# The head of a fused attention and expert kernel in another order, with the norm's statistics in a third piece

## The chip, the cores and the metric

The kernel runs as one program on one core of a Trainium2 chip. The metric is device time in microseconds. The kernel before has a median of 527.07 us over three runs, from 525.77 to 527.6.

## The reference

The reference is a gated cross-attention layer followed by a mixture-of-experts layer, all in 32-bit floats: 8 batches of 256 queries (`x`, width 256), 120 context rows per batch, 16 heads of 64, 8 experts with a hidden width of 1024, of which each token takes two.

```python
q = (layernorm(x) @ w_q).reshape(b, n, 16, 64)
k, v = split((ctx @ w_kv).reshape(b, m, 2, 16, 64))
out = softmax(einsum('bnhd,bmhd->bhnm', q, k) * 64 ** -0.5) @ v
x = x + tanh(g_xattn) * (out @ w_out + b_out)
probs = softmax(layernorm(x) @ Wr.T)            # 2048 tokens, 8 experts
gate = top-2 of probs, scaled to sum to one
y = sum over experts e of gate_e * (silu(xn @ W1[e].T) @ W2[e].T)
x = x + tanh(g_ffn) * y
```

## The kernel before, in words

Every 32-bit factor is split into a high part and a low part of 16 bits, and a product is three 16-bit products. ScalarE (ACT) makes the high parts, VectorE (DVE) or GpSimd (POOL) the low ones. The parts carry a power of two that is found on the chip: ACT or DVE takes a bound of a tensor (`weight_max`), PE spreads it (`attn_maxima`, bounds Actx, Awk, Awq, and A3 for the two that come last), and DVE makes the scale of it (`attn_scales`). The first batch doesn't wait for the split: its Q and K products take the 32-bit tensors as they are (`plain`, L1713).

Eight batches go through a software pipeline. Each engine has a loop `for p` (SP L511, POOL L741, ACT L1027, DVE L1565, PE L2020) whose body is a list of calls with an offset: `row_max(p + 2, 0)` acts on batch p + 2 in round p and does nothing outside 0 to 7. A function that works once returns where its batch is not 0. So the lists are an order written out by hand, and an engine runs its list strictly in that order; what it waits for are semaphores. The round of a batch is about 31 us long. The products share three banks (`j_bank`); four tables (`PRODUCT_ORDER`, `FULL_ORDER`, `HIGH_ORDER`, `FREE_ORDER`) tell in which order banks are taken, filled and freed, and from them come the semaphore counts.

What the change touches:

- `filler` (L1725): matmuls of a constant that keep PE busy. `x_T` (L1742) turns the normed queries of a batch; `x_high` (ACT, L833) and `x_low` (DVE, L1224) split them. For batch 0, `x_low` (L1245) leaves one 32-bit copy, `xn2T`. `q_product` and `k_product` make four parts of Q and two of K; `row_scores` (L1908) makes scores whose row maxima `row_max` (L1389) takes.
- `weight_sum` (ACT, L927): sums of squares of an expert's two weight matrices for the scale of their split, two instructions of 2048 elements each; `weight_diagonals` (L952) and the reduction of the spread sums (L1315) follow, and every split of these weights waits for them.
- `x_stats` (DVE, L1144 and L1147): mean and variance of the query tiles of 128 rows. There are 16: two for batch 0, then four, then ten.
- `norm_factors` (POOL, L565 to L573): eight small instructions that make scale and shift of the norm for the tiles of one piece. ACT norms batch b (L905) when its piece is done.
- `p_low` (POOL, L618): the low part of the softmax numerators, which PE's products with V wait for. `scatter` (L637): a batch's routes into a table in memory. `norm2_factors` (L647): the second norm's factors. POOL also makes low parts of the expert weights (L663 to L667).

```python
RESTS = ((NT, 4), (NT + 4, TT - NT - 4))      # tiles in the pieces after the first
SUMS = (1, 3,)                                # bounds that ACT takes as sums of squares
```

After the eighth round only the work on expert tiles is left, the last 29 of 39 in a loop of their own (`step`).

## Time and profile before

| | |
|---|---|
| median of three runs | 527.07 us (525.77 to 527.6) |
| the profiled execution | 530.4 us, of which the span is 528.7 us |
| mean granted TensorE clock | 0.983 |
| instructions | 17694 |
| PE busy | 486.9 us, 92% |
| DVE busy | 363.8 us, 69% |
| ACT busy | 371.2 us, 70% |
| POOL busy | 369.9 us, 70% |
| chain that ended last | PE 66%, POOL 12%, DVE 9%, ACT 5%, issue 5%, DMA 3% |

The span is the time between the first and the last instruction that the profiler saw; the profiled execution's time is 1.7 us more. Times on the timeline count from the span's start. The shares are means over stages that differ: up to some 75 us PE has gaps, afterwards hardly any, and from some 300 us on only expert tiles are left. Releasers are inferred, and a busy PE is not PE at its peak.

### The profile page before, as it was taken

Reading aid. Unit: us, or ns where it says so; the run is one execution under the profiler, and the core shown is the slowest. Engines: PE = TensorE matmul, PEld = TensorE weight load, DVE = VectorE, ACT = ScalarE, POOL = GpSimd, SP = SyncE. Lnnn points to the kernel's source line nnn. Section 1 sums busy time; section 2 is a strip of 40 time slices with the busy share of each in tenths; the row PEclk is TensorE's granted clock in tenths of the full one; section 3 lists DMA queues with packets and bytes.
Section 4 is the critical chain, followed back from the end, with each engine's and each line's share of the span. In section 5 each row is a group of like instructions: output and inputs, shape, how many; then the busy total and the mean of one; then the engine's idle time right before and its main releaser. Section 6 shows DMA issues by size and latency. Waiting matters only on the chain.

```text
span 528.7 us, 17694 instructions
## 1 busy us (share of the span) xinstructions
PE 486.9 (92%) x6692; PEld 436.4 (83%) x6692; DVE 363.8 (69%) x866; ACT 371.2 (70%) x577; POOL 369.9 (70%) x414
## 2 busy tenths in 40 slices
PE   2889689999999999999688999989999999999993
PEld 2877568888888878888468899979999999999993
DVE  5799899898988989998887757553344443444431
ACT  1788989999899989988764577544555655556551
POOL 5369779798999999899968766564554645455432
PEclk9999989999999999999989999998999999999998
DMA  7953416154360725325073638886888888788712
GB/s 289 398 195 95 167 38 204 51 185 140 99 208 34 243 67 182 124 95 195 24 268 110 255 118 303 251 254 150 260 226 245 241 226 265 212 256 239 211 22 31
DMA packets 35061, 94.87 MB, mean 179 GB/s; under 512 B 4507, under 2 KB 24475, under 8 KB 27645
## 3 DMA queue, kind: packets, MB, share of 16 engines
q1 hardware_dynamic: 25812, 82.79, 45.2%
q0 software_dynamic: 8592, 10.81, 11.9%
q8 instruction: 57, 0.93, 0.7%
q14 instruction: 24, 0.20, 0.1%
q10 hardware_dynamic: 576, 0.14, 0.1%
HBM read 74.45 MB, written 19.28 MB: 177 GB/s over the span
## 4 chain that ended last, share of the span: by engine, by line
PE 66%; POOL 12%; DVE 9%; ACT 5%; issue 5%; DMA 3%; POOLq 0%; SPq 0%; ACTq 0%; DVEq 0%
PE st_bank L1707 20%; PE j_bank L1707 15%; PE o_bank L1707 14%; PE j_bank L1852 4%; POOL pT L618 3%; POOL stage L663 3%; PE max_pair L1908 2%; PE j_bank L1713 2%; PE st_bank L1929 2%; POOL table L637 2%; PE j_bank L1811 2%; DMA stage<-in_w 2%; PE max_pair L1970 1%; DMA w2s<-in_wq 1%; PE j_bank L1876 1%
## 5 line engine op out<-in xcount | busy, mean ns | idle before, releaser
L1541 DVE SCALAR_TENSOR_TENSOR hT<-hf,h_scale,hT 128x512 f16<-128x512 f32 x78 | 58.9, 758 | 87.2 <-ACT hT L1016 87.1
L1707 PE MATMUL st_bank<-xsT,w_tile 128*128 128x128 f16 x1872 | 113.3, 221 | 2.1 <-DVE xsT L1535 1.4
L1707 PEld LDWEIGHTS st_bank<-xsT,w_tile 128*128 128x128 f16 x1872 | 109.6, 99 | 3.0 <-DVE xsT L1535 1.6
L730 POOL DMA_INDIRECT out<-yt,row_of x39 | 62.7, 1607 | 57.0 <-DVE yt L1550 42.3
L1010 ACT ACTIVATE hf<-st_bank,z_scale 128x512 f32<-128x512 f32 x78 | 52.9, 678 | 45.2 <-PE st_bank L1707 39.2
L618 POOL TENSOR_TENSOR pT<-pT 120x512 f16<-120x512 f32 x64 | 77.3, 1223 | 7.3 <-ACT pT L884 7.1
L1707 PE MATMUL o_bank<-w2s,hT 128*128 x600 | 69.7, 273 | 0.3 <-DVE yt L1550 0.3
L1016 ACT ACTIVATE hT<-hf,h_scale 128x512 f16<-128x512 f32 x78 | 56.3, 722 | 10.5 <-PE o_bank L1707 4.2
L1707 PEld LDWEIGHTS o_bank<-w2s,hT 128*128 128x128 f16 x600 | 57.6, 98 | 7.1 <-issue 0.8
L883 ACT ACTIVATE pT<-st_bank,exp_bias,logit_scale 120x512 f32<-120x512 f32 x64 | 50.0, 781 | 14.0 <-PE st_bank L1932 12.7
L663 POOL TENSOR_SCALAR stage<-stage,upw 128x512 f32<-128x512 f32 x32 | 56.5, 1766 | 4.1 <-ACT w_hi L983 4.1
L710 POOL DMA_INDIRECT xg<-xn,row_of x39 | 40.6, 1041 | 14.3 <-issue 11.0
L884 ACT ACTIVATE pT<-st_bank,exp_bias,logit_scale 120x512 f16<-120x512 f32 x64 | 50.1, 782 | 0.0
L1852 PE MATMUL j_bank<-wos,oT 128*128 128x256 f16 x384 | 45.5, 272 | 1.0 <-DVE oT L1224 1.0
L1707 PE MATMUL j_bank<-xnT,wqs 128*128 128x256 f16 x336 | 41.4, 274 | 1.7 <-DVE oT L1224 1.6
L1707 PE MATMUL o_bank<-v,pT 120*128 120x65 f16 x768 | 34.2, 194 | 8.4 <-DVE o L1412 5.5
L1707 PEld LDWEIGHTS o_bank<-v,pT 120*128 120x128 f16 x768 | 29.5, 98 | 15.0 <-issue 12.2
L991 ACT ACTIVATE xsT<-max_pair 128x256 f16<-128x256 f32 x39 | 14.8, 380 | 37.7 <-PE max_pair L1970 37.6
L1852 PEld LDWEIGHTS j_bank<-wos,oT 128*128 128x128 f16 x384 | 36.3, 98 | 5.3 <-DVE oT L1224 1.2
L637 POOL DMA_INDIRECT table<-entry,slot x32 | 32.2, 1005 | 11.0 <-issue 7.4
L1707 PE MATMUL j_bank<-w2s,hT 128*128 x336 | 39.0, 273 | 0.0
L1707 PEld LDWEIGHTS j_bank<-xnT,wqs 128*128 128x128 f16 x336 | 31.9, 98 | 6.5 <-DVE oT L1224 1.8
(226 smaller groups left out, 1022.7 us busy)
## 6 DMA issues: line engine op xcount, KB each, us to landing
w_tile<-w_split SPq DMA_DIRECT2D x39, 1024.0 KB, 6.3
stage<-in_w SPq DMA_DIRECT2D x16, 1024.0 KB, 5.1
w_split<-w_hi SPq DMA_DIRECT2D x8, 512.0 KB, 2.8
w_split<-stage SPq DMA_DIRECT2D x8, 512.0 KB, 3.8
out<-x SPq DMA_DIRECT2D x17, 128.0 KB, 3.2
xin<-in_x SPq DMA_DIRECT2D x8, 256.0 KB
w2s<-in_wkv SPq DMA_DIRECT2D x2, 1024.0 KB, 11.9
xres<-in_x SPq DMA_DIRECT2D x16, 128.0 KB, 2.1
```

Of the source, the lines that this page charges most:

```text
L618: pool.tensor_tensor(pT[g % 2][:, 1, h, :], pT32[:, h, :], pT[g % 2][:, 0, h, :], ALU.subtract).then_inc(pT_low[h], 1)
L637: pool.indirect_dma_start(out=table[:], out_offset=bass.IndirectOffsetOnAxis(slot[b % 2][:, t, k:k + 1], 0), in_=entry[b % 2][:, t, k, :], ...
L663: chain.link(pool.tensor_scalar(chunk, chunk, upw[q % 2][:, i:i + 1], None, ALU.mult))
L710: pool.indirect_dma_start(out=xg[t % XG][:], out_offset=None, in_=xn2_dram[0:rows], in_offset=bass.IndirectOffsetOnAxis(row_of[:, t:t + 1] ...
L730: pool.indirect_dma_start(out=out[0:rows], out_offset=bass.IndirectOffsetOnAxis(row_of[:, t:t + 1], 0), in_=yt[t % XG][:], in_offset=None, ...
L883: nc.scalar.activation(pT32[:, h, :], st_bank[h][0:M, :], ACT.Exp, bias=exp_bias[0:M], scale=logit_scale[0:M])
L884: nc.scalar.activation(pT[g % 2][:, 0, h, :], st_bank[h][0:M, :], ACT.Exp, bias=exp_bias[0:M], scale=logit_scale[0:M]).then_inc(exp_done[h ...
L1010: nc.scalar.activation(hf[par][:, cols], z_bank[a][:], ACT.Silu, scale=z_scale[:, bass.ds(t, 1)]).then_inc(silu_done, 1)
L1016: nc.scalar.activation(hT[par][:, 0, 4 * a:4 * a + 4, :], hf[par][:, cols].rearrange("p (c n) -> p c n", c=4), ACT.Copy, scale=h_scale[:, ...
L1541: nc.vector.scalar_tensor_tensor(out=hT[par][:, 1, 4 * a:4 * a + 4, :], in0=hf[par][:, 512 * a:512 * a + 512].rearrange("p (c n) -> p c n" ...
L1707: ins = pe.matmul(out, lhs[i](a), rhs[i](c), start=(i == 0 and a + c == 0), stop=(i == n - 1 and a == 1))
L1852: ins = pe.matmul(dst[:, 0:D], oT[t][:, a, ic, :], wos[:, c, ic, :], start=(ic + a + c == 0), stop=(ic == IC - 1 and a == 1))
```

## The change

- PE's head: 100 fillers first, then the queries of batch 0 are turned, and the bounds Awq, Actx and Awk are spread each with one Q product of batch 0 behind it. K's product and the first scores follow; A3 comes later, behind the transposition of the second batch's queries.
- DVE, ACT and POOL follow that order in the head: DVE takes its 32-bit copy of the turned queries ahead of its constants, and the row maxima of the first scores, the bound of the output weights and several low parts ahead of A3's scale. The bound of the context moves from DVE to ACT, where it becomes a sum of squares (`SUMS`). POOL's memset of the pads waits for the scale of `w_q`, and a quarter of the context's low part moves ahead of the first norm factors.
- ACT: `x_high` stands ahead of both `weight_sum`s, in every round.
- The third piece of the norm is split in two: four tiles at its old place, and the last six later. DVE's statistics for them come in round 1, behind `norm2_rows(0)`, POOL's factors in round 2, among the first scatters.
- The tables of banks have entries of their own for batch 0. From round 6 on the lists are written out without a loop, in the same order.

On PE, at the program's start; `o_bank<-onesb` is a filler, `w2s,onesb` the spreading of a bound, `ident,xin` the transposition, `xn2T,w2s` the Q products, `xn_0,w2s` K's. Before:

```order
L1725 MATMUL o_bank<-onesb 128x128 x12
L1838 MATMUL j_bank<-w2s,onesb 128x128
L1742 MATMUL j_bank<-ident,xin 128x128 x4
L1725 MATMUL o_bank<-onesb 128x128 x40
L1838 MATMUL j_bank<-w2s,onesb 128x128
L1725 MATMUL o_bank<-onesb 128x128 x16
L1838 MATMUL j_bank<-w2s,onesb 128x128
L1713 MATMUL j_bank<-xn2T,w2s 128x256 x12
L1713 MATMUL j_bank<-xn_0,w2s 128x120 x16
L1838 MATMUL j_bank<-w2s,onesb 128x256
L1908 MATMUL max_pair<-kT,qT 128x120 x24
```

And now:

```order
L1901 MATMUL o_bank<-onesb 128x128 x100
L1918 MATMUL j_bank<-ident,xin 128x128 x4
L2012 MATMUL j_bank<-w2s,onesb 128x128
L1889 MATMUL j_bank<-xn2T,w2s 128x256 x4
L2012 MATMUL j_bank<-w2s,onesb 128x128
L1889 MATMUL j_bank<-xn2T,w2s 128x256 x4
L2012 MATMUL j_bank<-w2s,onesb 128x128
L1889 MATMUL j_bank<-xn2T,w2s 128x256 x4
L1889 MATMUL j_bank<-xn_0,w2s 128x120 x16
L2082 MATMUL max_pair<-kT,qT 128x120 x24
```

Two of the three Q products now stand ahead of the last of the three bounds, one behind it, and A3 (128x256) is gone from ahead of the scores.

On DVE in round 1, behind the copy of the first batch's turned second norm (`xn2T<-j_bank`). Before:

```order
L1226 SCALAR_TENSOR_TENSOR qT<-j_bank,qT 128x512
L1309 COPY xn2T<-j_bank 128x512
L1409 RECIPROCAL rsum<-o_bank 128x4
L1412 TENSOR_TENSOR o<-o_bank,rsum 128x2x2x64
L1226 SCALAR_TENSOR_TENSOR qT<-j_bank,qT 128x512
L1335 MAX top<-j_bank 128x8 x2
```

And now:

```order
L1331 SCALAR_TENSOR_TENSOR qT<-j_bank,qT 128x512
L1414 COPY xn2T<-j_bank 128x512
L1249 BN_STATS stats<-w2s 128x6 x6
L1252 BN_AGGR mv<-stats 128x2 x6
L1514 RECIPROCAL rsum<-o_bank 128x4
L1517 TENSOR_TENSOR o<-o_bank,rsum 128x2x2x64
L1331 SCALAR_TENSOR_TENSOR qT<-j_bank,qT 128x512
L1440 MAX top<-j_bank 128x8 x2
```

Twelve instructions on six tiles stand between the copy and the attention's work.

On POOL in round 2, at the first batch's scatters (`table<-entry,slot`). Before:

```order
L618 TENSOR_TENSOR pT<-pT 120x512
L637 DMA table<-entry,slot 16512x16 x2
L618 TENSOR_TENSOR pT<-pT 120x512
L637 DMA table<-entry,slot 16512x16 x2
L647 TENSOR_SCALAR ln_b<-mv 128x2
```

And now:

```order
L626 TENSOR_TENSOR pT<-pT 120x512
L645 DMA table<-entry,slot 16512x16 x2
L626 TENSOR_TENSOR pT<-pT 120x512
L572 TENSOR_SCALAR ln_a<-mv 128x6
L573 TENSOR_TENSOR ln_a<-ln_a,minus_half 128x6
L574 TENSOR_TENSOR ln_a<-ln_a 128x6
L575 TENSOR_TENSOR ln_a<-ln_a 128x6
L576 TENSOR_SCALAR ln_a<-ln_a 128x6
L577 TENSOR_SCALAR ln_a<-mv 128x6
L579 TENSOR_TENSOR ln_scale<-ln_a 128x6
L580 TENSOR_TENSOR ln_shift<-ln_a,ln_scale 128x6
L645 DMA table<-entry,slot 16512x16 x2
```

Eight instructions on six columns stand between a low part and the second pair of scatters, and all that follows on POOL comes behind them.

The core of the diff:

```diff
-RESTS = ((NT, 4), (NT + 4, TT - NT - 4))
-SUMS = (1, 3,)
+RESTS = ((NT, 4), (NT + 4, 4), (NT + 8, TT - NT - 8))
+SUMS = (0, 1, 3)
...
-PRODUCT_ORDER = (("Awq", 4), ("Q3", 2), ("X2T", -1), ("Q1", 2), ("LG", -1), ("FE", -2), ("Ka", 2), ("Vb", 1), ("OT0a", 0),
+PRODUCT_ORDER = (("XTf", 4), ("Awq", 4), ("Q3", 2), ("X2T", -1), ("Q1", 2), ("LG", -1), ("FE", -2), ("Ka", 2), ("Vb", 1), ("OT0a", 0),
...
-            sp.dma_start(x_rest[1], x_v[:, RESTS[1][0]:sum(RESTS[1]), :]).then_inc(x_all_in[1], 16)
+            for i in range(1, len(RESTS)):
+                sp.dma_start(x_rest[i], x_v[:, RESTS[i][0]:sum(RESTS[i]), :]).then_inc(x_all_in[i], 16)
...
+                pool.wait_ge(up_done[2], 1)
                 pool.memset(pad, 0.0).then_inc(pool_chain, 1)
...
                 p_low(p + 6, 2, 1)
+                norm_factors(p + 6, 2)
+                norm_factors(p + 4, 3)
                 scatter(p + 4, 1)
...
+                weight_low(p + 8, 0, 0, 0, 1)
                 norm_factors(p + 8, 1)
-                weight_low(p + 8, 0, 0)
+                weight_low(p + 8, 0, 0, 1, WEIGHT_PARTS)
...
-                norm_factors(p + 7, 2)
                 p_low(p + 7, 2, 0)
...
                 exps(p, 2, 1)
+                x_high(p + 2)
                 weight_sum(p + 1, 0)
-                x_high(p + 2)
...
                 x_stats(p + 1, 2)
                 norm2_rows(p - 1)
+                x_stats(p - 1, 3)
...
+                first_x_low(p + 3)
+                constants(p + 3)
                 attn_scales(p + 3, 0)
+                first_q_low(p + 3, 0)
...
                 row_max(p + 2, 0)
+                weight_max(p + 2, 4)
...
+            def first_x_T(b):
+                if b == 0:
+                    filler(100)
+                    x_T(b)
+
+            def first_q(b, i):
+                if b == 0:
+                    q_product(b, i)
...
-                attn_maxima(p + 2, 3)
...
-                x_T(p + 3)
+                x_T(p + 3 if p > -3 else B)
+                attn_maxima(p + 2, 3)
...
+                first_q(p + 3, 0)
                 attn_maxima(p + 3, 0)
+                first_q(p + 3, 3)
```

## Rows read from the trace of the kernel before

**Rows 1.** Chain of waits: start us, us on the chain, what.

```profile
74.52 2.79 PE j_bank L1707 x24
...
177.55 1.35 POOL w2s L667
```

**Rows 2.** Busy time in windows: stretch, length, five engines, PEclk, DMA, GB/s.

```profile
80.00:100.00 20.00, 20.00 (x305) 17.33 (x302) 17.72 (x44) 18.90 (x31) 15.54 (x20) 1.00 0.48 156
122.00:178.00 56.00, 54.60 (x822) 47.60 (x820) 50.71 (x126) 51.75 (x81) 52.28 (x55) 1.00 0.39 125
28.20:38.50 10.30, 8.85 (x138) 7.20 (x139) 9.89 (x20) 8.91 (x12) 7.35 (x6) 1.00 0.55 190
62.90:66.20 3.30, 0.73 (x14) 0.47 (x14) 2.68 (x6) 3.21 (x7) 0.87 (x1) 1.00 0.00 0
68.00:69.00 1.00, 1.00 (x3) 0.22 (x1) 0.96 (x3) 0.84 (x3) 0.82 (x2) 0.50 0.00 0
```

**Rows 3.** Timeline of the head: start us, us, engine, line, operation, [idle before <-releaser].

```profile
13.31 1.91 ACT L938 ACTIVATE w_hi<-w2s 128x2048 f16<-128x2048 f32 x1 [3.14 <-DMA w2s<-in_wkv]
...
16.51 1.06 PE L1725 MATMUL o_bank<-onesb 128*128 128x128 bf16 x16
...
17.40 0.22 PE L1838 MATMUL j_bank<-w2s,onesb 128*128 128x128 bf16 x1
...
19.10 5.42 PE L1713 MATMUL j_bank<-xn2T,w2s 128*128 128x256 f32 x24 [1.48 <-DVE xn2T L1245]
...
24.07 2.28 DVE L1155 TENSOR_REDUCE amax<-w2s 128x1 f32<-128x2048 f32 x1
...
24.36 3.73 PE L1713 MATMUL j_bank<-xn,w2s 128*128 128x120 f32 x32
...
28.12 0.80 PE L1908 MATMUL max_pair<-kT,qT 64*128 64x120 f16 x24
...
38.51 1.28 DVE L1212 SCALAR_TENSOR_TENSOR wkvs<-w2s,up,wkvs 128x1024 f16<-128x1024 f32 x1
```

**Rows 4.** Timeline of 45 to 66 us, DVE and ACT.

```profile
45.45 3.35 DVE L1144 BATCH_NORM_STATS2 stats<-w2s 128x6 f32<-128x256 f32 x10
...
48.84 0.78 DVE L1147 BATCH_NORM_AGGREGATE mv<-stats 128x2 f32<-128x6 f32 x10
...
50.10 0.60 ACT L850 ACTIVATE v<-j_bank 120x512 f16<-120x512 f32 x1 [1.20 <-PE j_bank L1713]
...
60.92 1.96 ACT L927 ACTIVATE w2s<-stage 128x2048 f16<-128x2048 f32 x1
...
63.49 0.69 DVE L1224 TENSOR_TENSOR xnT<-j_bank,xnT 128x512 f16<-128x512 f32 x1 [2.26 <-ACT xnT L833]
...
65.44 0.70 ACT L952 ACTIVATE diag<-ident,amc 128x128 bf16<-128x128 f32 x2
```

**Rows 5.** Timeline of 106 to 114 us, DVE and PE.

```profile
106.51 0.68 DVE L1309 COPY xn2T<-j_bank 128x512 f32<-128x512 f32 x1
...
112.43 0.68 DVE L1224 TENSOR_TENSOR oT<-j_bank,oT 128x512 f16<-128x512 f32 x1
...
113.44 1.42 PE L1707 MATMUL j_bank<-ctxs,wkvs 128*128 128x120 f16 x24
```

**Rows 6.** Timeline of POOL, with one PE row.

```profile
57.52 0.27 POOL L565 TENSOR_SCALAR ln_a<-mv 128x10 f32<-128x10 f32 x1
...
61.49 2.27 POOL L618 TENSOR_TENSOR pT<-pT 120x512 f16<-120x512 f32 x2
...
122.13 1.22 POOL L637 DMA_INDIRECT table<-entry,slot  x1 [0.55 <-DVE entry L1369]
...
128.35 0.23 POOL L647 TENSOR_SCALAR ln_b<-mv 128x2 f32<-128x2 f32 x1
...
130.93 2.72 POOL L618 TENSOR_TENSOR pT<-pT 120x512 f16<-120x512 f32 x2
...
133.75 0.53 PE L1707 MATMUL o_bank<-v,pT 120*128 120x65 f16 x12 [0.73 <-issue]
```

More of the change, by code:

```diff
@@ L127, in positions @@
     @staticmethod
-    def positions(order, without=None):
+    def positions(order):
         at = {}
@@ L137, in bank @@
     def bank(self, name, b):
-        return self.taken[name, b] % JOB_BANKS
+        return self.taken[job(name, b), b] % JOB_BANKS
     def fulled(self, name, b):
-        return self.full[name, b] + 1
+        return self.full[job(name, b), b] + 1
     def highed(self, name, b):
-        return self.high[name, b] + 1
+        return self.high[job(name, b), b] + 1
     def freed(self, name, b):
-        return self.free[name, b] + 1
+        return self.free[job(name, b), b] + 1
 JOBS = Jobs()
@@ L667, in split_low, with weight_low @@
                     pool.tensor_tensor(w2_part(q, 1, c), chunk, w2_part(q, 0, c), ALU.subtract).then_inc(w2_low[k], 1)
-            def weight_low(b, i, j):
+            def weight_low(b, i, j, first, last):
                 if b:
@@ L678, in weight_low @@
                 n = (hi - lo) // WEIGHT_PARTS
-                for c in range(0, hi - lo, n):
+                for c in range(first * n, last * n, n):
                     part = raw[:, :, c:c + n]
@@ L977, in split_high @@
                     elif q < 6:
-                        for j in range(2):
+                        for j in range(len(RESTS)):
                             act.wait_ge(stats_done[j], 1)
@@ new lines, in _ @@
+            exps(6, 1, 0)
+            o_high(5, 1, 1)
+            exps(6, 1, 1)
+            o_high(5, 0, 1)
+            k_high(7, 1)
+            gate_ratio(4)
+            q_high(7, 2)
+            exps(6, 2, 0)
+            exps(6, 2, 1)
+            weight_sum(7, 0)
+            weight_sum(7, 1)
+            weight_diagonals(7)
+            exps(6, 3, 0)
+            exps(6, 3, 1)
+            split_high(7, 0, 0)
+            o_high(6, 1, 0)
+            v_high(7, 0)
+            split_high(7, 0, 1)
@@ new lines, in _ @@
+            norm2(5)
+            split_high(7, 1, 1)
+            exps(7, 0, 0)
+            exps(7, 0, 1)
+            split_high(7, 1, 0)
+            v_high(7, 1)
+            o_high(6, 0, 0)
+            exps(7, 1, 0)
+            o_high(6, 1, 1)
+            exps(7, 1, 1)
+            o_high(6, 0, 1)
+            gate_ratio(5)
+            exps(7, 2, 0)
+            exps(7, 2, 1)
+            exps(7, 3, 0)
+            tile_high(7, 0)
+            exps(7, 3, 1)
+            tile_high(7, 1)
@@ new lines, in _ @@
+            split_low(7, 0, 2)
+            norm2_rows(5)
+            norm_o(6, 3, 1)
+            choose(5)
+            row_max(7, 3)
+            row_ids(4, 0)
+            tile_experts(4, 0)
+            v_low(7, 1)
+            o_low(6, 0, 0)
+            norm_o(7, 0, 0)
+            split_low(7, 1, 1)
+            o_low(6, 1, 1)
+            max_rows(7, 1)
+            split_low(7, 1, 0)
+            norm_o(7, 0, 1)
+            tile_scales(7, 0, 0)
+            o_low(6, 0, 1)
+            slots(5)
@@ new lines, in _ @@
+            tile_T(7, 0)
+            tile_T(7, 1)
+            spare('OT1a', 7, 44)
+            values(7, 2, 0)
+            tile_up(7, 0, 0)
+            o_T(7, 1, 0)
+            tile_up(7, 0, 1)
+            values(7, 2, 1)
+            tile_up(7, 1, 0)
+            values(7, 3, 0)
+            norm2_T(6)
+            values(7, 3, 1)
+            logits(6)
+            o_T(7, 0, 0)
+            o_T(7, 1, 1)
+            tile_up(7, 1, 1)
+            o_T(7, 0, 1)
+            ranks(6)
+            out_product(7, 1, 0)
@@ new lines, in _ @@
+            out_product(7, 1, 1)
+            out_product(7, 0, 0)
+            tile_T(7, 2)
+            out_product(7, 0, 1)
+            tile_T(7, 3)
+            tile_down(7, 0)
+            tile_up(7, 2, 0)
+            tile_T(7, 4)
+            tile_down(7, 1)
+            tile_T(7, 5)
+            norm2_T(7)
+            tile_up(7, 2, 1)
+            logits(7)
+            tile_up(7, 3, 0)
+            tile_up(7, 3, 1)
+            ranks(7)
+            tile_down(7, 2)
+            tile_up(7, 4, 0)
```

499 lines of the change are left out of this document (298 added, 201 removed).

## The prediction, on record before the changed kernel ran

> **What bounds the kernel now.** I read the chain of waits first. Its last piece on PE before the stage in which PE is full is the group of Q products at 74.52 us; from there it runs over PE and, from 122 us on, over POOL's splits of the expert weights, of which the last is at 177.55 [rows 1]. Then I read busy time by windows [rows 2]. Between 80 and 100 us PE is busy 20.00 of 20 us. Between 122 and 178 PE is busy 54.60 of 56 and POOL 52.28, and POOL's gaps there are short waits at scatters such as the 0.55 at 122.13 [rows 6]. So the kernel has three stages that matter here: a head to about 75 us in which PE has gaps (0.73 us busy between 62.9 and 66.2), a stage in which PE is full, and one in which PE and POOL are both nearly full. What is won in the head is carried through the later stages, since they have no slack to swallow it and nothing in them waits for a fixed time. What is added to an engine in the later stages is paid unless a slack is there in that place.
>
> In the head DVE and ACT set the pace: from 28.2 to 38.5 DVE is busy 9.89 of 10.30 us and ACT 8.91, PE 8.85 [rows 2]. Behind 50 us it is ACT: it waits 1.20 us for a V product at 50.10 [rows 4], and in the window at 63 us it is busy 3.21 of 3.30 while DVE is 2.68 and POOL 0.87.
>
> **The head, to the low part at 38.51.** K's product of the first batch needs the bound of the K weights. They land at 13.31 us, after ACT waited 3.14 for the transfer, and the bound is spread at 17.40 [rows 3]. Neither moves: the transfer and ACT's pass over it are the same. But before, three Q products stood between bound and K, 5.42 us for 24 records, and they started only at 19.10, because DVE made their operand late. Now two of them come before the bound and one is left behind it: 5.42 / 3 = 1.81. So K starts at about 17.4 + 0.2 (the spreading) + 1.8 and some wait for the scale, which I put at 0.3: 19.7 instead of 24.36. From K's start to the end of the first scores before is 28.12 + 0.80 - 24.36 = 4.56 us, of which some 0.2 was A3's spreading, which is now later. The first row maxima can thus start at 19.7 + 4.4 = 24.1. Behind them DVE has the same set of work as before from 28.2 to 38.5, which is 10.30, and the bound of the output weights (2.28 at 24.07 [rows 3]) with its diagonal of some 0.2, which moved behind the row maxima: 24.1 + 10.3 + 2.5 = 36.9. The same low part starts at 38.51 before. That is **-1.6 us**. The other edits of the head are in that set: the bound of the context goes from DVE to ACT, where a wait of 3.14 for a transfer hides it, and the memsets and the quarter of a low part on POOL stand where POOL has a gap.
>
> **The split of the statistics, its gain.** Ten tiles cost DVE 3.35 + 0.78 = 4.13 us at 45.45 and 48.84 [rows 4]; four cost 0.4 of it, 1.65, so DVE saves 2.48 there. It is not all gain, since ACT limits this stretch: what ACT can use of it is the 1.20 that it waited for the V product at 50.10, which stands behind DVE's work. I take **-1.2**; the bounds are 0 and -2.5.
>
> **The high part ahead of the weight sums.** The transposed queries' high part stood behind a sum of 1.96 us at 60.92, and DVE waited 2.26 for it at 63.49. Now DVE gets it earlier, but the two sums still have to be done on ACT before the diagonals at 65.44 [rows 4], for which the weights' split waits, and they come no earlier: ACT does the same work in another order. I take **0**, with bounds 0 and -2.3.
>
> **The statistics' six tiles in round 1.** They cost 0.6 of 4.13 = 2.5 us in one piece on DVE, directly behind the copy at 106.51 [rows 5]. PE is full there, and what DVE does next frees the banks into which PE writes. The slimmest place shown is that of a low part that ends at 112.43 + 0.68 = 113.11 and frees a bank for the K product at 113.44: a slack of 0.33 us. A slack of that size leaves 2.5 - 0.3 = 2.2 of the burst for PE to wait; some of DVE's idle time is in between (the copy's end at 107.19 to the next operation), so I take **+2.0**. The bounds are 0, if PE can go on with work whose banks are free, and 2.5.
>
> **The factors' eight instructions in round 2.** Two sizes are in the trace: eight instructions on two columns take 130.93 - 128.35 = 2.58 us, on ten columns 61.49 - 57.52 = 3.97 [rows 6]. Six columns lie midway: 3.3. POOL is nearly full from 122 us on, and PE waits for it: 0.73 us at 133.75 for the low parts that ended just before [rows 6]. Behind the eight instructions stand the second pair of scatters, the second norm's factors, the low parts for which PE waits there, and the weights' splits on which the chain of waits ends. I take **+3.3**; the bounds are 0, if POOL's own slack is larger than it looks, and 3.3. The piece at the old place shrinks from ten columns to four, which saves at most a microsecond there, but POOL has gaps in that stretch (0.87 of 3.30 busy at 63 [rows 2]), so it gives nothing.
>
> **The sum.** -1.6 - 1.2 + 0 + 2.0 + 3.3 = +2.5 us. Against the profiled execution, 530.4 us (a span of 528.7 and 1.7 around it), this makes 532.9. That execution lies 3.3 us above the median of 527.07, and the median is what the next runs are like, so I forecast 527.07 + 2.5 = 529.6.
>
> **The rivals.** *Both moved pieces are hidden (faster).* The mechanism is that POOL's eight instructions displace nothing that PE needs at once: they stand behind the low part of 122 us and before scatters whose result is read rounds later, and the low parts behind them could come 2.6 us later than now if the engines ahead of PE had that much stored. Then DVE's burst is taken up in the same way, and only the head's -2.8 is left: 524.3. For it speaks that PE's wait in this place is only 0.73 us; against it that POOL has no more than 56 - 52.28 = 3.7 us of gaps in the whole stretch [rows 2]. It decides if PE's waits for low parts in round 2 stay under one microsecond.
>
> *All gains of the head add (no change).* If DVE, not ACT, sets the pace to 75 us, the 1.6 of the head, the 2.5 of the statistics and the 2.3 of the high part add to 6.4, and with the 5.3 that the moved pieces cost the time is 527.07 - 6.4 + 5.3 = 526.0. For it speaks DVE's wait of 2.26; against it ACT's 3.21 of 3.30 in the same window. If the gains add and the pieces are hidden too, it would be 520.7; I give that little.
>
> *The head's PE slows down (slower).* Now PE does its 100 fillers in one piece at the start: at the 1.06 us for 16 of [rows 3] they take 6.6 us and end before the queries are there to be turned, and a gap follows in which PE has next to nothing. The row of 62.9 to 66.2 shows such a gap, and in the row of 68 to 69 the granted clock is 0.50, the lower of its two levels, 1.2 GHz of 2.4 [rows 2]. If that happens before the Q and K products, the Q product behind the bound takes 1.81 more, and the head's 1.6 is gone. Then the sum is -1.2 + 5.3 = +4.1, or 531.2. The Trainium skill has a rule on this ("TensorE: Matmul & The Clock Gate", Part 1: The HAM clock gate): the clock follows how busy the engine has lately been, and an engine that pauses goes back to half rate. The trace agrees with it in those two windows. By that rule alone the gap behind the fillers would decide for this rival; against it stands that the bounds and Q products now follow one another closely.
>
> **How the numbers follow.** What one measurement of this kernel can't tell from no change is about 0.3%, 1.6 us: faster is below 525.5, slower above 528.7. My forecast gets 0.37, with its own range from 528.4 to 530.8; the hidden pieces 0.21, the gains that add 0.24, the slow clock 0.12, and both hidden and adding 0.06. Faster: 0.21 + 0.06 and 0.04 from the edge of the adding gains, 0.31. Same: 0.20 from the adding gains and 0.03 from my forecast's lower edge, 0.23. Slower: 0.34 and 0.12, 0.46. The range from 523.6 to 531.6 leaves out 520.7 and the outer halves of the hidden pieces' and slow clock's cases, which is just under 2 in 10.
>
> **What would show it right or wrong.** Right: the first row maxima on DVE at about 24 instead of 30.3 us, and the first low part of the K and V weights at about 37; the Q products of 74.52 at about 71.7; six statistics at about 104 us followed by waits of PE that sum to about two; on POOL, between the scatters of the first batch, eight small instructions of 3.3 us in all and behind them a wait of PE for a low part of some 3 us more than 0.73. Wrong in the head: a granted clock of 0.5 around the first K product, or DVE idle in front of the first row maxima; a start of the Q products before 69 us would show that the gains add. Wrong in the later stages: PE busy without a break from 104 to 140 us, with waits under one microsecond; then the moved pieces cost nothing and the kernel is faster.

## The result, and the profile after

The changed kernel takes 542.62 us (median of four, 537.18 to 544.05) where the kernel before takes 527.34 beside it. By these medians it is slower by 15.3 us where 2.5 were forecast. The ratio, 1.0267 with an interval from 1.0205 to 1.0329, is taken over fast runs alone, without one of 535.82 us of the kernel before, and stands for some 14 us. The profiled execution is the longest of the four, 544.05 us, its span 542.3, its mean granted TensorE clock 0.971 instead of 0.983.

Busy time by windows of the changed kernel, the two stretches of [rows 2] that tell the stages apart:

```profile
80.00:100.00 20.00, 19.58 (x298) 17.14 (x297) 17.21 (x42) 17.70 (x30) 15.16 (x20) 1.00 0.50 159
122.00:178.00 56.00, 51.03 (x704) 43.45 (x699) 43.67 (x110) 45.61 (x70) 47.07 (x58) 0.94 0.32 108
```

PE was busy 54.60 of 56 us between 122 and 178; now it is 51.03, at a clock of 0.94, and POOL 47.07 instead of 52.28. The changed kernel is up to 10 us late in this window, so less of its work falls into it (704 instructions on PE instead of 822), and PE, which was nearly full, stands idle for 5 us of it.

To see where time goes when nothing but the order is changed, I took landmarks: the starts of DVE's reductions of the row maxima (32 in a run), and DVE's results of the expert tiles (`yt`, 39). The first column is the start in the kernel before in us, the others are differences from it, all from the traces. The second trace is another execution of the kernel before; the variants are told of below.

| landmark in before | second trace | after | no_split | stats_early | factors_behind | pe_kept_busy | head_only | xT_earlier |
|---|---|---|---|---|---|---|---|---|
| 30.3 | -0.7 | -4.2 | -3.6 | -3.8 | -4.6 | -3.4 | -3.3 | -4.7 |
| 40.9 | -0.7 | 0.0 | +0.6 | +0.4 | -0.4 | +0.8 | +0.9 | -0.5 |
| 79.9 | -0.7 | +0.1 | +1.1 | +0.9 | 0.0 | +1.3 | +0.2 | 0.0 |
| 99.7 | -0.7 | +0.7 | +1.6 | +1.5 | +0.6 | +1.8 | +0.1 | +0.1 |
| 109.6 | -0.7 | +3.6 | +2.4 | +2.2 | +3.5 | +4.8 | +0.1 | +0.1 |
| 129.9 | -0.7 | +3.7 | +2.8 | +2.7 | +3.5 | +4.8 | +0.1 | +1.2 |
| 140.5 | -0.7 | +9.2 | +2.9 | +7.9 | +3.6 | +7.4 | +0.1 | +0.6 |
| 160.7 | -0.7 | +10.2 | +3.6 | +8.9 | +5.6 | +8.0 | +0.1 | +1.9 |
| 245.7 | -1.2 | +12.2 | +5.5 | +10.9 | +8.1 | +9.9 | -0.2 | +3.0 |
| 309.2, first `yt` | -3.1 | +9.5 | +2.8 | +8.9 | +7.1 | +7.3 | -0.4 | +1.1 |
| 344.5, seventh `yt` | -3.1 | +15.5 | +7.0 | +14.6 | +11.7 | +9.1 | +3.4 | +5.4 |
| 520.7, last `yt` | -4.7 | +13.8 | +5.3 | +13.0 | +10.1 | +9.1 | +1.7 | +3.9 |

Read the third column downwards. The head's gain of 4.2 us is there at the first row maxima and gone at the third. 2.9 us are lost between 99.7 and 109.6, 5.5 between 129.9 and 140.5, some 3 in small steps up to 245.7, and 6 between the first and the seventh tile. The first trace of the kernel before is itself 4.7 us later at the end than the second, all but 0.7 of it behind 180 us, so the end of the table is less sure than its top.

### The profile page after: what moved, and what is told of

Its sections match the earlier page's. It is cut to its first block, busy times and chain, and to the rows that moved or that the text cites. A ratio compares the mean times of both kernels' runs of the same rounds, so it can differ in the third digit from the quotient of the medians.

```text
span 542.3 us, 17776 instructions
## 1 busy us (share of the span) xinstructions
PE 496.9 (92%) x6724; PEld 441.3 (81%) x6724; DVE 362.6 (67%) x866; ACT 374.1 (69%) x580; POOL 371.6 (69%) x422
## 4 chain that ended last, share of the span: by engine, by line
PE 57%; POOL 10%; ACT 10%; DVE 10%; issue 7%; DMA 5%; POOLq 1%; ACTq 0%; DVEq 0%
PE j_bank L1883 16%; PE st_bank L1883 16%; PE o_bank L1883 11%; ACT w2s L969 4%; POOL table L645 3%; PE max_pair L2082 2%; PE j_bank L1889 2%; PE j_bank L2026 2%; DMA out<-yt,row_of 2%; PE st_bank L2103 2%; POOL pT L626 2%; PE j_bank L1987 1%; ACT w_hi L1025 1%; POOL xg L719 1%; DMA xg<-xn,row_of 1%
## 5 line engine op out<-in xcount | busy, mean ns | idle before, releaser
L926 ACT ACTIVATE pT<-st_bank,exp_bias,logit_scale 120x512 f16<-120x512 f32 x64 | 50.1, 783 | 0.0
L1883 PE MATMUL j_bank<-xnT,wqs 128*128 128x256 f16 x336 | 43.9, 284 | 1.5 <-DVE oT L1329 1.5
L1883 PEld LDWEIGHTS j_bank<-xnT,wqs 128*128 128x128 f16 x336 | 33.4, 102 | 7.9 <-DVE oT L1329 1.8
```

The lines of the kernel that those rows point to most:

```text
L926: nc.scalar.activation(pT[g % 2][:, 0, h, :], st_bank[h][0:M, :], ACT.Exp, bias=exp_bias[0:M], scale=logit_scale[0:M]).then_inc(exp_done[h ...
L1883: ins = pe.matmul(out, lhs[i](a), rhs[i](c), start=(i == 0 and a + c == 0), stop=(i == n - 1 and a == 1))
```

## The head

Timeline of the changed kernel's head, the answers to [rows 3], and the window of its first Q product (columns as there and in [rows 2]):

```profile
13.24 3.51 PE L1889 MATMUL j_bank<-xn2T,w2s 128*128 128x256 f32 x8 [1.90 <-DVE xn2T L1350]
...
14.68 1.91 ACT L980 ACTIVATE w_hi<-w2s 128x2048 f16<-128x2048 f32 x1 [1.41 <-DMA w2s<-in_wkv]
...
18.80 0.23 PE L2012 MATMUL j_bank<-w2s,onesb 128*128 128x128 bf16 x1 [0.21 <-DVE qT L1331]
...
21.46 3.83 PE L1889 MATMUL j_bank<-xn,w2s 128*128 128x120 f32 x32 [0.60 <-DVE qT L1331]
...
26.07 1.17 DVE L1494 TENSOR_REDUCE max_pair<-max_pair 128x8 f32<-128x960 f32 x1 [1.27 <-PE max_pair L2082]
...
38.45 1.28 DVE L1317 SCALAR_TENSOR_TENSOR wkvs<-w2s,up,wkvs 128x1024 f16<-128x1024 f32 x1
```

```profile
14.00:16.00 2.00, 2.00 (x7) 1.55 (x6) 0.00 (x0) 1.32 (x1) 1.71 (x5) 0.50 1.04 387
```

Behind the fillers PE paused 1.90 us, the granted clock was 0.50 (1.2 GHz) at 14 to 16, and the first Q product took 3.51 us. The sum over the K weights began at 14.68, not 13.31, since the transfer landed later (the sum begins at 14.46 to 15.20 in the 14 traces with the new head and at 13.28 to 14.30 in the six with the old one; why is open), and the bound of K stands on PE behind the second Q product: 18.80 instead of 17.40. So the row maxima began at 26.07 and not at 24.1. From there to the low part at 38.45 it is 12.4 us, of which DVE is busy 11.85, much as worked out (12.8).

**head_filled** puts fillers where PE paused.

```diff
 def first_q(b, i):
     if b == 0:
+        if i == 0:
+            filler(30)
         q_product(b, i)
```

> The changed kernel with 30 fillers between the first bound and the first Q product in the head. Theory of the clock: that Q product took 3.51 us at a granted clock of 0.5 where 1.8 is its time at full clock, and the spreading of the bounds stands behind it; kept busy, K's product starts 1.6 us earlier, the first row maxima start at about 24.5 instead of 26.07 us and the median falls by 0 to 1.6 us. Rival, that the head waits for the transfer of the K weights: the row maxima stay at 26 us and the median at 542.6.

```profile
11.01 1.84 PE L1901 MATMUL o_bank<-onesb 128*128 128x128 bf16 x30
13.08 1.96 PE L1889 MATMUL j_bank<-xn2T,w2s 128*128 128x256 f32 x8 [0.23 <-DVE xn2T L1350]
...
18.22 0.23 PE L2012 MATMUL j_bank<-w2s,onesb 128*128 128x128 bf16 x1 [1.34 <-DVE qT L1331]
...
25.50 1.17 DVE L1494 TENSOR_REDUCE max_pair<-max_pair 128x8 f32<-128x960 f32 x1 [1.27 <-PE max_pair L2082]
```

539.24 us (538.42 to 543.11). The timeline of this variant shows the Q product at 1.96 instead of 3.51 us: that was the clock. But only 0.6 us of the 1.6 reach the row maxima, for PE now waits 1.34 for DVE to free a bank. DVE had waited 1.03 for ACT there, which was at the sum over the K weights from 14.46 to 16.37, as soon as their transfer had landed: by this chain the rest is the rival's. The expected 24.5 was missed. The median is 3.4 us below the changed kernel's, more than was expected, but the intervals overlap (1.0187 to 1.0302 here, 1.0205 to 1.0329 there); what this trace shows at 138 us is told with the late tiles.

**head_only** has the new head alone: the late tiles in one piece and the high part back behind the first weight sum (the diffs of the next two sections reversed).

> The kernel with the new head alone: the late tiles in one piece of ten, and the high part of the turned queries behind the first weight sum again. The variant with head and high part ran at 535.3 against 528.2 us before. Theory that the head itself costs, since its pauses of PE put the granted clock to 0.5 at 12 to 18 us and again near 66: the median stays at 533 to 536. Rival, that the high part ahead of the weight sums costs (the sums of the third expert start 3 us later than before at 92 us): it falls to 528 to 530.

532.23 us (529.88 to 533.19) beside 526.85: 1.0098, 1.0067 to 1.013. This was between the two expectations, and its column in the table says why neither holds: from 80 to 250 us it is level with the kernel before. The new head gains and loses nothing there. What it loses lies behind 309 us.

**head_kept** adds fillers in three pauses of the head, **head_kept2** a fourth group ahead of the sixth batch's `norm2_T`, and **before_kept** has the fourth group alone, in the kernel before.

```diff
+        keep_busy({-2: 24, -1: 24}.get(p, 0))     # fillers, beside filler(30) as above
         weight_maxima(p + 2)
...
     dst = bank_free("X2T", b)                     # norm2_T; head_kept2 and before_kept
+    for _ in range(24 if b == 5 else 0):
+        pe.matmul(dst[:, 0:P], onesb[:], onesb[:], start=True, stop=True)
```

> The kernel with the new head alone (late tiles in one piece, the high part behind the first weight sum) with PE kept busy in three pauses: 30 fillers ahead of the first Q product, 24 each ahead of the products that spread the weight sums at 36 and 66 us. The head alone ran at 532.2 against 526.9 before, with a granted clock of 0.5 at 12 to 18 us. Theory of the clock: no stretch at 0.5 below 80 us is left and the median is 527 to 530. Rival, that the head loses by its order and the clock is a side effect: 531 to 533.

> The kernel before with 24 fillers ahead of the transposition of the sixth batch's second norm, where PE paused 1.48 us at 259 us and the granted clock was 0.5 from 262 to 268 in the profiled execution. Theory of the clock: that stretch goes and 2 to 3 us with it where an execution has it, 524 to 526 us. Rival, that the fast executions of the kernel before don't have this stretch (the profiled one lies 3.3 us above the median): no change, 526.5 to 528.

> The new head alone with PE kept busy in the three pauses of the head and in the one of the sixth batch's second norm. Theory of the clock: the gain of both adds, 524 to 528 us, at or below the kernel before. Rival: 530 or more.

head_kept: 527.52 us (525.23 to 530.46), a ratio of 0.9995 (0.9968 to 1.0021). head_kept2: 527.9, 0.9997 (0.9963 to 1.003). before_kept: 530.53, 1.0044 (1.0019 to 1.007), slower instead of faster. The trace of before_kept goes from -0.5 at 257.0 us to -2.4 at the first `yt`, and the second trace of the kernel before goes from -1.2 to -3.1 without any filler: nothing is gained there, as the rival had it. By medians the fillers give head_only its 5 us back, as the theory of the clock had it. By the traces they don't do so in the head, as further executions show.

**before_again, before_again2, head_only_again, head_kept_again** are further executions of kernels that are told of above.

> The kernel before, unchanged, for a second profiled execution. Theory that its first profiled execution (530.4 against a median of 527) was a slow one in the stretch of 250 to 370 us, with a granted clock of 0.5 at 262 to 268 and 358: this one has at most one such stretch there, reaches the first expert tile's result by 306 us instead of 309, and takes 526 to 528 us. Rival, that the profile itself costs 3 us: 530 again, with the same stretches.

> The same once more, for the spread of one kernel's traces: the landmarks up to 250 us within 0.5 us of the first profiled execution if the loss lies behind 250 us alone; otherwise up to 3 us apart already at 80 us, by the clock of the stretch at 62 to 72 us.

> The new head alone, unchanged, for a second profiled execution. In the first its row maxima from 80 to 160 us lay 0.1 us behind the kernel before, though its median is 5.4 us above. Theory that the clock in the stretch of 62 to 72 us, which was full in that execution, decides: with a clock of 0.5 there the row maxima at 80 us are 2 to 4 us behind. Rival, that the loss lies behind 250 us, in the waits for the expert tiles' transfers: 0.1 us behind at 80 us again, and 3 to 5 at 350.

> The new head alone with PE kept busy in three pauses, unchanged, for a second profiled execution. The first was 2.8 us behind the kernel before at 80 us, with a clock of 0.5 at 66 to 70 us in spite of the fillers, and even with it at the end. Theory of the clock: where the stretch at 66 us is at full clock, it is 1 us ahead at 80 us, as the variant with a fourth group of fillers was; else 2.8 behind.

The profiled executions took 525.45, 526.22, 531.62 and 528.94 us. The medians are as before: 526.76 and 526.67 for the kernel before, 531.92 (1.0104, 1.0062 to 1.0146) for head_only and 527.83 (0.9981, 0.9942 to 1.0019) for head_kept. The second and third traces of the kernel before lie within 0.8 us of the first up to 180 us and 4.0 to 4.7 ahead at the end: the first lost these 4 us behind 180 us, and a profiled execution need not be longer than the others. head_only_again is 1.1 us ahead of the first trace of before at 100 us, head_kept_again 1.0: the fillers win nothing up to there. So the rival is nearer, that head_only loses behind 250 us. The difference between the two is mainly one place, at the seventh tile: head_only_again goes from -3.4 at the sixth to +1.4 there, and head_kept_again stays at -1.2. The wait, in timelines of the changed kernel, no_split and head_only_again:

```profile
353.91 0.44 PE L2144 MATMUL max_pair<-ident,xg 128*128 128x128 f32 x2 [2.75 <-DMA xg<-xn,row_of]
```

```profile
347.03 0.44 PE L2142 MATMUL max_pair<-ident,xg 128*128 128x128 f32 x2 [2.33 <-DMA xg<-xn,row_of]
```

```profile
339.82 0.44 PE L2142 MATMUL max_pair<-ident,xg 128*128 128x128 f32 x2 [2.87 <-DMA xg<-xn,row_of]
```

PE waits 2.3 to 2.9 us for rows gathered for a tile. Behind the wait of head_only_again the granted clock is 0.50 at 342 to 344, so that the place costs 4.7 us; in the first trace of head_only the clock stays full, and it costs 2.3. None of the three traces of the kernel before has this wait, nor the two of head_kept; both of head_only have it, and before_kept, whose only edit is 24 fillers, has it too (1.95 us). But so has head_kept2, whose median is level with the kernel before, in an execution of 530.33 us:

```profile
339.74 0.44 PE L2148 MATMUL max_pair<-ident,xg 128*128 128x128 f32 x2 [2.66 <-DMA xg<-xn,row_of]
```

The kernel before has next to nothing to spare here either: in its third trace the rows land 5.0 us after POOL issues this gather at 332.57, and PE takes them at 337.69. In head_only_again the issue is at 332.95 and the landing 6.8 us later. So the wait comes with edits that don't touch the tiles, and not with the edit alone; what makes the gather land later is open.

## The high part ahead of the weight sums

Timeline of ACT in the round of 92 us, first of the changed kernel, then of head_only, where the high part stands behind the first sum:

```profile
93.26 0.60 ACT L875 ACTIVATE xnT<-j_bank 128x512 f16<-128x512 f32 x1 [1.45 <-PE j_bank L1918]
93.76 1.90 ACT L969 ACTIVATE w2s<-stage 128x2048 f16<-128x2048 f32 x1
...
97.94 0.70 ACT L994 ACTIVATE diag<-ident,amc 128x128 bf16<-128x128 f32 x2
```

```profile
91.68 1.92 ACT L968 ACTIVATE w2s<-stage 128x2048 f16<-128x2048 f32 x1
...
93.58 0.60 ACT L874 ACTIVATE xnT<-j_bank 128x512 f16<-128x512 f32 x1
...
94.05 1.93 ACT L968 ACTIVATE w2s<-stage 128x2048 f16<-128x2048 f32 x1
...
96.16 0.70 ACT L993 ACTIVATE diag<-ident,amc 128x128 bf16<-128x128 f32 x2
```

ACT works in order. With the high part first, it stands idle 1.45 us until PE has turned the queries, and only then begins the sums; the diagonals come 1.8 us later than in head_only. Behind the first sum, the high part finds its operand ready.

**x_high_only** makes this edit in the kernel before.

```diff
+                x_high(p + 2)
                 weight_sum(p + 1, 0)
-                x_high(p + 2)
```

> The kernel before with one edit: the high part of the turned queries ahead of both weight sums in every round. Theory that the head costs: this alone changes nothing, 527 to 529 us, DVE's wait of 2.26 at 63 us is gone, and the weight sums start up to 0.6 us later in each round. Rival: the sums are late in each round, POOL's and ACT's splits of the weights with them, and the median is 531 to 535.

535.02 us (533.63 to 536.27) beside 526.85: 1.015, 1.0133 to 1.0167. The rival holds: the edit that I priced at nothing costs 8 us by itself in the old head, where PE turns the second batch's queries late:

```profile
34.55 0.60 ACT L833 ACTIVATE xnT<-j_bank 128x512 f16<-128x512 f32 x1 [2.52 <-PE j_bank L1742]
35.05 1.90 ACT L927 ACTIVATE w2s<-stage 128x2048 f16<-128x2048 f32 x1
...
40.07 0.27 PE L1828 MATMUL j_bank<-diag,onesb 128*128 128x258 bf16 x1 [2.69 <-ACT diag L952]
```

In the new head the first of these waits is 0.16 us, and the edit costs less: no_split is at 535.31 and head_only at 532.23, 3.1 us apart, or 1.7 when each is taken against the kernel before beside it (528.23 and 526.85), where the intervals overlap (1.0104 to 1.019 and 1.0067 to 1.013). By the traces no_split is 5.7 us behind head_only at 245.7 us, 3.3 at the first `yt` and 3.6 at the last.

**xT_earlier** is no_split with PE's transposition one product earlier (the two entries in `FULL_ORDER` are exchanged with it).

```diff
-                out_product(p, 1, 1)
                 x_T(p + 3 if p > -3 else B)
+                out_product(p, 1, 1)
```

> The changed kernel with the late tiles in one piece and, on PE, the transposition of the next queries one product earlier in each round (ahead of the second half of the first output product, 1.48 us). The high part stays ahead of the weight sums. Theory that the high part costs because ACT, which works in order, waits 1.45 us at 94 us for that transposition before it can start the sums: the wait shrinks under 0.2 us in each round, the sums start about 1.4 us earlier, and the median falls from 535.3 to 532 to 533, where the same kernel with the high part behind the first sum is. Rival, that the sums are late by the 0.6 us of the high part itself: 534.5 to 536.

534.92 us (530.39 to 536.49): the median does not fall. But the timeline tells the theories apart within one execution:

```profile
91.88 0.60 ACT L874 ACTIVATE xnT<-j_bank 128x512 f16<-128x512 f32 x1 [0.17 <-PE j_bank L1916]
...
122.55 0.66 PE L1916 MATMUL j_bank<-ident,xin 128*128 128x128 f32 x4 [1.06 <-DVE qT L1330]
...
123.32 0.60 ACT L874 ACTIVATE xnT<-j_bank 128x512 f16<-128x512 f32 x1 [1.54 <-PE j_bank L1916]
```

In the round of 92 us the wait is 0.17, and the table shows no loss there (0.0 to +0.1 from 79.9 to 109.6, where no_split goes from +1.1 to +2.4). From 122 us on the transposition itself waits 1.06 for a bank that DVE frees, ACT waits 1.54 again, and the loss is back (+1.2 at 129.9, +3.0 at 245.7). That the wait, not the length of the high part, is what costs is shown for that round; the median can't show it.

**xT_earlier_kept**, the same with head_kept's fillers:

> The same with PE kept busy in the three pauses of the head (30 fillers ahead of the first Q product, 24 each ahead of the products that spread the weight sums at 36 and 66 us). If the theories of ACT's wait and of the clock both hold, head and high part together cost nothing, and DVE's wait of 2.26 us at 63 us, which the high part takes away, is a gain: 524 to 528 us, at or below the kernel before. Rival: 530 or more.

528.94 us (527.32 to 533.09), 1.0032 (1.0007 to 1.0056): between both expectations, and slightly slower than the kernel before. DVE's wait, which the edit shortens from 2.26 to 0.35 us, brought nothing that the medians show.

## The six late tiles

**no_split** leaves the late tiles in one piece.

```diff
-RESTS = ((NT, 4), (NT + 4, 4), (NT + 8, TT - NT - 8))
+RESTS = ((NT, 4), (NT + 4, TT - NT - 4))
...
-                norm_factors(p + 4, 3)
...
-                x_stats(p - 1, 3)
```

> The changed kernel with the norm's later tiles in one piece of ten again (statistics and factors at the earlier place), all else as changed. First theory, that the six late tiles make the whole loss, by DVE's burst (+2.9 us seen between the row maxima at 100 and 113 us) and POOL's eight instructions with the slow clock behind them (+6.2 us seen between 134 and 150): the row maxima of the fourth batch come within 1 us of the kernel before and the median is 526 to 531 us. Rival, that the new head and the reordered high parts cost by themselves: the median stays above 535 us.

535.31 us (535.12 to 535.86), 1.0147 (1.0104 to 1.019). The split costs 7.3 us, or 8.2 against the kernel before beside each: about half of the loss, and the rival has the other half.

The statistics' gain is missing in this comparison too. In the changed kernel the landmark at 50.1 us comes 3.0 us earlier than in no_split, the one at 59.6 only 0.4, which it had from the start. ACT and PE of the changed kernel there:

```profile
48.40 1.93 PE L1889 MATMUL j_bank<-w2s,xn 128*120 128x512 f32 x4
50.37 0.60 ACT L892 ACTIVATE v<-j_bank 120x512 f16<-120x512 f32 x1 [1.20 <-PE j_bank L1889]
...
65.92 0.70 ACT L994 ACTIVATE diag<-ident,amc 128x128 bf16<-128x128 f32 x2
```

ACT waits the same 1.20 us for the V product as before ([rows 4]) and as in no_split. This product follows other products on PE without a gap, so it does not come earlier when DVE is done sooner, and from it to the diagonals ACT has no pause in which it could use what DVE saves.

DVE and PE in round 1 of the changed kernel, timeline, the answer to [rows 5]:

```profile
107.97 0.68 DVE L1414 COPY xn2T<-j_bank 128x512 f32<-128x512 f32 x1
...
108.57 2.05 DVE L1249 BATCH_NORM_STATS2 stats<-w2s 128x6 f32<-128x256 f32 x6
...
110.66 0.51 DVE L1252 BATCH_NORM_AGGREGATE mv<-stats 128x2 f32<-128x6 f32 x6
...
112.35 1.50 PE L1883 MATMUL j_bank<-wkvs,ctxs 128*120 128x512 f16 x6 [1.09 <-DVE qT L1331]
```

The burst is 2.56 us, and PE waits for the bank that DVE frees behind it.

**stats_early** puts the six statistics back behind the four.

```diff
                 x_stats(p + 1, 2)
+                x_stats(p + 1, 3)
...
-                x_stats(p - 1, 3)
```

> The changed kernel with the statistics of the six tiles at once behind those of the four, as in the kernel before; POOL's factors of the six stay late. First theory: the burst on DVE costs 2.9 us by itself, so the median falls from 542.6 to 539 to 541 us and the wait of 3.3 us of PE behind the factors stays. Rival, that the burst is taken up where PE waits for POOL anyway: no change, 542 to 543.

538.41 us (537.72 to 543.33), 4.2 below the changed kernel by medians, though the intervals overlap (1.0165 to 1.0252 against 1.0205 to 1.0329). In the traces 2.9 us from 99.7 to 109.6 become 0.7: the burst is worth 2.2 us there, and PE's wait behind the factors stays at 3.32, as the theory has it. Against the changed kernel's trace it is 0.8 behind at 79.9 and 1.3 ahead at 245.7. The profiled execution was the longest of the five, 543.33.

POOL and PE in round 2 of the changed kernel, timeline, and the clock behind the wait; these answer to [rows 6]:

```profile
129.16 0.26 POOL L572 TENSOR_SCALAR ln_a<-mv 128x6 f32<-128x6 f32 x1
...
132.30 0.20 POOL L580 TENSOR_TENSOR ln_shift<-ln_a,ln_scale 128x6 f32<-128x6 f32 x1
...
137.68 2.27 POOL L626 TENSOR_TENSOR pT<-pT 120x512 f16<-120x512 f32 x2
...
140.05 0.82 PE L1883 MATMUL o_bank<-v,pT 120*128 120x65 f16 x12 [3.33 <-issue]
140.68 2.75 PE L1883 MATMUL j_bank<-xnT,wqs 128*128 128x256 f16 x12
...
144.07 2.45 PE L1883 MATMUL j_bank<-xnT,wqs 128*128 128x256 f16 x12
```

```profile
140.00:142.00 2.00, 1.95 (x19) 1.61 (x20) 1.06 (x3) 0.05 (x1) 1.92 (x2) 0.50 0.00 0
142.00:144.00 2.00, 2.00 (x11) 1.69 (x10) 1.29 (x2) 0.47 (x1) 2.00 (x2) 0.50 0.00 0
```

The eight instructions take 3.3 us, as worked out, and PE waits 3.33 for the low part behind them instead of 0.73. The prediction ended there. But behind this pause the granted clock is 0.50, and the next products take 2.75 and 2.45 us.

**pe_kept_busy** fills that pause.

```diff
+                if p == 2:
+                    dst = bank_free("Q3", p + 2)
+                    for _ in range(54):
+                        pe.matmul(dst[:, 0:P], onesb[:], onesb[:], start=True, stop=True)
                 values(p, 3, 0)
```

> The changed kernel with 54 fillers on PE in round 2 ahead of the product with V that waits 3.3 us behind POOL's factors; they write a free bank and use no result. Theory of the clock: the 3.3 us in which PE pauses put the granted clock to 0.5 behind it, and two Q products take 2.75 and 2.45 us instead of 1.48; kept busy, they take 1.5 each, and the median falls by about 3 us to 539 to 540. Rival, that only the queue on POOL costs: the fillers change nothing, 542 to 543.

```profile
138.11 3.19 PE L2209 MATMUL j_bank<-onesb 128*128 128x128 bf16 x54 [0.26 <-DVE oT L1329]
141.18 0.53 PE L1883 MATMUL o_bank<-v,pT 120*128 120x65 f16 x12
141.54 1.48 PE L1883 MATMUL j_bank<-xnT,wqs 128*128 128x256 f16 x12
```

536.99 us (534.16 to 539.43), 5.6 below, more than was expected. In the timeline the Q product takes 1.48 us, and the loss from 129.9 to 140.5 is 2.6 instead of 5.5 us. So of these 5.5 some 2.9 are the clock, and 2.6 POOL's queue. The rest of the 5.6 is not from here: at the first `yt` this trace is 2.2 us ahead of the changed kernel's, and 6.4 at the seventh, where its wait for gathered rows is shorter (1.52 instead of 2.75).

The trace of head_filled gives the same price without a filler in this pause. PE waits as long, but in that execution the clock stays full:

```profile
139.31 0.53 PE L1883 MATMUL o_bank<-v,pT 120*128 120x65 f16 x12 [3.32 <-issue]
139.67 1.48 PE L1883 MATMUL j_bank<-xnT,wqs 128*128 128x256 f16 x12
```

```profile
140.00:142.00 2.00, 2.00 (x21) 1.84 (x19) 1.97 (x4) 0.76 (x2) 1.92 (x3) 1.00 0.00 0
```

It loses 2.6 us from 129.9 to 140.5, as pe_kept_busy does. So the 2.9 us of the clock are paid in some executions and not in others (the changed kernel's and stats_early's traces have them).

**factors_behind** moves the eight instructions behind the two low parts.

```diff
-                norm_factors(p + 4, 3)
                 scatter(p + 4, 1)
...
                 p_low(p + 6, 3, 1)
+                norm_factors(p + 4, 3)
```

> The changed kernel with POOL's eight instructions for the six late tiles moved behind the two low parts of the softmax numerators for which PE waited 3.3 us, ahead of the splits of the expert weights; DVE's burst, the head and the high part stay. Theory that PE's wait for that low part and the slow clock behind it are the cost: the wait of 3.3 us shrinks under one microsecond, no stretch at a granted clock of 0.5 follows, and the median falls from 542.6 to 537 to 539 us. Rival, the prediction's own step, that POOL is full and everything behind the eight instructions is 3.3 us late wherever they stand: the splits of the weights pass it on, and the median stays at 541 to 543.

538.96 us (538.01 to 540.41), 3.7 below by medians. No loss is left from 129.9 to 140.5 (+0.1), and the wait is gone. But 2.0 us come back by 160.7: the low parts of the next pair on POOL are late in their turn, here by 1.02 us of PE's time:

```profile
136.37 0.57 POOL L572 TENSOR_SCALAR ln_a<-mv 128x6 f32<-128x6 f32 x1
136.50 0.54 PE L1883 MATMUL o_bank<-v,pT 120*128 120x65 f16 x12
...
148.30 0.52 PE L1883 MATMUL o_bank<-v,pT 120*128 120x65 f16 x12 [1.02 <-issue]
```

no_split loses 0.6 in the same stretch, so about half of POOL's 2.6 us is paid later. So both expectations hold in part: the wait and its clock go, and a full POOL passes on some of what is added to it.

## Fillers in the wrong place

**no_split_filled** and **x_high_filled** were to fill the pause at 64 us. The 40 fillers that they put ahead of `weight_maxima` of the third expert ran a round later, at 97 to 103 us, where PE is full; no_split_filled also has 30 in the head and 24 that did hit the pause.

```diff
+        keep_busy({-1: 24, 0: 40}.get(p, 0))      # no_split_filled, beside filler(30)
         weight_maxima(p + 2)
```

> The changed kernel with the late tiles in one piece, and with PE kept busy in three pauses of the head: 30 fillers ahead of the first Q product, 24 and 40 ahead of the products that spread the weight sums in the rounds of 35 and 65 us. Theory of the clock: the stretches at a granted clock of 0.5 at 12 to 18 and 66 to 72 us are gone, the row maxima at 100 us come 2 to 4 us earlier than in the variant without fillers, and the median falls from 535.3 to 530 to 533. Rival, that the pauses themselves cost and the clock doesn't: no change.

> The kernel before with the high part ahead of the weight sums, and 40 fillers in the free bank of the product that spreads the second expert's sums, at about 64 us. Theory of the clock: the half clock that the kernel before has at 66 to 71 us is gone and with it about 2 us: 525 to 526, below the kernel before. Rival: what is won at 70 us is lost in a later wait, 527 to 529.

x_high_filled: 538.51 us (535.66 to 540.52), 3.5 above x_high_only, for these fillers (timeline):

```profile
100.80 2.40 PE L1828 MATMUL j_bank<-onesb 128*128 128x128 bf16 x40
```

2.40 us of added work in the full stage cost about that much (2.7 to 5.9 in its landmarks between 91.9 and 99.7, where x_high_only has 3.0 and 3.5). As a test of the clock it failed; as a price of PE's full stage it is what the prediction assumed. no_split_filled: 532.11 us (531.08 to 533.9), 3.2 below no_split in spite of the same price (1.8 when each is taken against the kernel before beside it). Its windows against those of no_split, no_split first:

```profile
10.00:26.00 16.00, 12.96 (x69) 10.67 (x71) 10.20 (x38) 11.94 (x15) 8.72 (x17) 0.79 1.03 402
62.00:74.00 12.00, 9.03 (x99) 6.82 (x97) 8.71 (x16) 10.79 (x16) 10.44 (x13) 0.72 0.02 5
```

```profile
10.00:26.00 16.00, 12.80 (x117) 10.90 (x117) 11.23 (x38) 12.10 (x15) 9.11 (x18) 1.00 1.03 403
62.00:74.00 12.00, 9.15 (x141) 7.46 (x137) 10.57 (x20) 11.50 (x16) 10.45 (x13) 1.00 0.01 1
```

The clock is full in both stretches, and the landmark at 79.9 comes 2.0 us earlier (-0.9 instead of +1.1), of which 0.4 is there at the first landmark already.

## Why the prediction was wrong

The sign was right, for the two terms above zero were real; the sum was 2.5 where the runs show 15.3. Step by step:

- **The head, -1.6: failed.** The step "Neither moves" is wrong: K's weights are summed 1.4 us later, and K's bound is spread behind a Q product, 1.4 us later too. K's product starts at 21.46 and not at 19.7, and at 38.5 us 0.06 us is left. DVE's work of 12.8 (12.4 measured) was right; its start was not.
- **The statistics' gain, -1.2: failed.** A landmark at 50.1 us is 2.4 us earlier, at 59.6 nothing is left. The term took it that ACT's 1.20 us for the V product stands behind DVE's work; it stands behind PE's, and stays 1.20.
- **The high part, "0, with bounds 0 and -2.3": failed, and on the other side.** I looked at the one place where DVE waited for ACT. I did not look at what ACT itself waits for in the new order, in every round, and who stands behind it. It costs 1.7 to 3.1 us by medians with the new head, 3.6 by the traces, and 8 with the old one.
- **DVE's burst, +2.0: right.** 2.2 us by the traces in its stretch.
- **POOL's eight instructions, +3.3: right in size, short by the clock.** They are 3.3 us long, PE waits 3.33 instead of 0.73, which is 2.6 more, and the clock behind the wait adds some 2.9 in the executions in which it falls.
- **The slow clock as a rival, 0.12:** it came, at 14 to 16 us as described, but in the profiled execution also at 36 to 40, 60 to 71 and 138 to 146, where I had not placed it (the kernel before has it at 66 to 71 too). It should have been a term, with a chance, beside each new wait of PE, not a case of its own. The rule quoted with it from the Trainium skill ("TensorE: Matmul & The Clock Gate", Part 1: The HAM clock gate), that a pausing engine goes back to half rate, agrees with the changed kernel's trace at 140 us, 0.50 behind a pause of 3.33, and not with head_filled's, 1.00 behind 3.32.
- **"Nothing in them waits for a fixed time": failed.** On the expert tiles PE waits for rows that a transfer brings: 6 of the changed kernel's us are lost between the first and the seventh tile, and none of the three traces of the kernel before has that wait.

By medians, each against the kernel before beside it, the parts are: head 5.4, high part 1.7, split 8.2. They are differences along one chain of variants and add to the 15.3 by construction; each is uncertain by two to three us. The head's 5.4 is not explained by anything up to 250 us; it comes with the wait at the seventh tile, whose cause is open.

The traces up to 245.7 us, ahead of the tiles, divide the changed kernel's +12.2 in this way: head_only is at -0.2 and no_split at +5.5, so some 5.7 go with the high part. The other 6.7 are the six late tiles: 2.2 for DVE's burst, 2.6 for POOL's queue, 2.9 for the clock behind it, less the 0.9 by which the changed kernel is ahead of no_split at 79.9.

## What to carry to other kernels

Where an instruction moves ahead in an in-order queue, ask first what it waits for at its new place, in each round, and what stands behind it: a wait that was hidden behind two sums became the engine's own. Price a pause of PE at the pause and, as a case with a chance, the slow products behind it. And take more than one trace before a few us at the end of a long chain are put down to an edit.

## What was not expected of the hardware

- One pause of 3.33 us cost about 2.9 us more in products at a clock of 0.50. Filling it with 54 matmuls that nobody reads took these 2.9 us away; in another execution a pause of 3.32 us left the clock at 1.00.
- Behind a pause of 1.76 us at 64 to 66 us the clock was 0.50 in all three traces of the kernel before and in one of head_kept, and full in both of head_only and in the other of head_kept; the two of head_kept are 3.7 us apart at 80 us.
- A wait of 2 to 3 us for a gathered tile at 340 us appears in both traces of head_only and in none of the kernel before, whose tile code is the same; head_kept2 has it and head_kept has not.
